# PEER stage of a decoder on one core: two of a tile's eight products of weights and activations on GpSimd instead of VectorE

## The reference

```python
q = (x @ Wq + bq).reshape(B, S, N_HEADS, D_QUERY)
s1 = jnp.einsum('bshd,nd->bshn', q1, K1)
s2 = jnp.einsum('bshd,nd->bshn', q2, K2)
v1, i1 = jax.lax.top_k(s1, TOPK)
v2, i2 = jax.lax.top_k(s2, TOPK)
...
vals, best = jax.lax.top_k(all_scores, TOPK)
expert_idx = jnp.take_along_axis(all_indices, best, axis=-1)
w_down = W_down[expert_idx]
w_up = W_up[expert_idx]
scores = jax.nn.softmax(vals, axis=-1)
h = jnp.einsum('bsd,bshkd->bshk', x, w_down)
h = jax.nn.gelu(h, approximate=False) * scores
out = jnp.einsum('bshk,bshkd->bsd', h, w_up)
```

## Time and profile before

| | |
|---|---|
| median of 3 runs | 3761.95 us (3757.82 to 3762.19) |
| profiled execution | 3762.07 us |
| its span | 3760.3 us |
| mean granted TensorE clock | 0.937 |
| busy over the span | PE 3271.3 (87%), PEld 2778.2 (74%), DVE 2726.7 (73%), ACT 1199.3 (32%), POOL 2150.9 (57%) |
| PEER's macros | about 972 to 2493 us of the span |

### The profile page before, as it was taken

The page is one execution under the profiler, slowest core; times in us unless marked ns, Lnnn a source line. Parts: engine busy times, 40 slices in busy tenths (PEclk is TensorE's granted clock), DMA queues, the critical chain, the costliest instruction groups (busy, mean ns, idle before and its releaser), DMA issues. The chain is left out here.

```text
span 3760.3 us, 93455 instructions
## 1 busy us (share of the span) xinstructions
PE 3271.3 (87%) x33694; PEld 2778.2 (74%) x33695; DVE 2726.7 (73%) x10805; ACT 1199.3 (32%) x3136; POOL 2150.9 (57%) x2456
## 2 busy tenths in 40 slices
PE   6999957876599999999999999978888799799998
PEld 4777735554488888888888888855555577699998
DVE  6666634544999999999999999948888467433333
ACT  1443425543222222222222222216665222122221
POOL 4444325551577777777777777768887233233333
PEclk9999978998799999999999999989999789799999
DMA  5444434443000000000000000024453231566665
GB/s 154 112 106 110 110 83 111 123 113 131 1 2 2 2 2 2 2 2 2 2 2 2 2 2 2 2 70 124 122 127 99 70 106 52 141 181 182 181 181 134
DMA packets 256260, 277.91 MB, mean 74 GB/s; under 512 B 44145, under 2 KB 200817, under 8 KB 255345
## 3 DMA queue, kind: packets, MB, share of 16 engines
q1 hardware_dynamic: 242225, 253.69, 23.5%
q0 software_dynamic: 13632, 18.91, 3.5%
HBM read 187.63 MB, written 72.29 MB: 69 GB/s over the span
## 5 line engine op out<-in xcount | busy, mean ns | idle before, releaser
L1190 POOL TENSOR_TENSOR peer_hot_v<-peer_hot_e,peer_parts 80x512 bf16<-80x512 bf16 x768 | 991.1, 1317 | 321.2 <-DVE peer_hot_e L1233 311.6
L1009 PE MATMUL peer_ps_u<-peer_up,peer_g 128*128 128x256 f32 x2048 | 533.5, 407 | 0.6 <-DVE x_all L1331 0.6
L990 PEld LDWEIGHTS peer_ps_h<-peer_xnT,peer_down 128*128 128x128 f32 x4096 | 513.4, 197 | 16.0 <-DMA peer_down<-in_peer_down 1.2
L990 PE MATMUL peer_ps_h<-peer_xnT,peer_down 128*128 128x128 f32 x4096 | 512.9, 280 | 1.0 <-DMA peer_down<-in_peer_down 1.0
L1000 PE MATMUL peer_ps_w<-peer_hot_v,peer_hot_u 80*128 80x32 bf16 x12288 | 347.3, 177 | 145.3 <-DVE peer_g L1245 98.6
L1000 PEld LDWEIGHTS peer_ps_w<-peer_hot_v,peer_hot_u 80*128 80x128 bf16 x12288 | 337.1, 97 | 167.4 <-issue 90.9
L1009 PEld LDWEIGHTS peer_ps_u<-peer_up,peer_g 128*128 128x128 f32 x2048 | 392.6, 201 | 53.2 <-issue 1.0
L1087 ACT ACTIVATE peer_g<-peer_ps_h 128x512 f32<-128x512 f32 x256 | 152.9, 597 | 842.3 <-PE peer_ps_h L990 842.0
L1237 DVE TENSOR_TENSOR peer_hot_u<-peer_count,peer_uvT 80x2048 bf16<-80x2048 bf16 x256 | 349.4, 1365 | 0.0
L2160 POOL DMA_INDIRECT out<-moe_y,moe_target x71 | 112.6, 1585 | 312.5 <-DVE moe_y L2261 309.6
L2104 PE MATMUL moe_ps_t<-moe_xgT,moe_w 128*128 128x128 f32 x2272 | 267.4, 276 | 0.0
(11 more groups left out here) (370 smaller groups left out, 7107.8 us busy)
## 6 DMA issues: line engine op xcount, KB each, us to landing
moe_w<-in_moe_w SPq DMA_DIRECT2D x142, 512.0 KB, 4.5
causal_qs<-causal_qscratch SPq DMA_DIRECT2D x32, 384.0 KB, 4.0
cross_qs<-cross_qscratch SPq DMA_DIRECT2D x32, 384.0 KB, 3.6
band_qs<-band_qscratch SPq DMA_DIRECT2D x32, 384.0 KB, 4.0
route_w<-in_moe_w SPq DMA_DIRECT2D x8, 1024.0 KB, 5.9
causal_qscratch<-causal_part SPq DMA_DIRECT2D x32, 192.0 KB, 2.6
causal_kscratch<-causal_part SPq DMA_DIRECT2D x32, 192.0 KB, 2.0
causal_ks<-causal_kscratch SPq DMA_DIRECT2D x32, 192.0 KB, 4.3
```

The source lines that it names most:

```text
L990: mm = nc.tensor.matmul(ps_h[:, n % 2, k * P:(k + 1) * P], down[:, c, 4 * n + k, :], xnT[:, par, c, :], start=(c == 0), stop=(c == DC - 1))
L1009: mm = nc.tensor.matmul(ps_u[:], g[:, par, v, :], up[:, v, :], start=(v == 0), stop=(v == EV - 1))
L1190: ins = nc.gpsimd.tensor_tensor(hot_v[0:SEL, n % RING, part], hot_e[0:SEL, n % RING], w, ALU.mult)
```

## The change

DVE's `weigh` returns at once for chunks 2 and 5 (`APART`). For these, ACT copies PE's bank to `wcopy` in SBUF (`take_w`), since POOL reads SBUF here, as the first thing of its turns 3 and 6. POOL's new `weigh` multiplies the copy into `g`, behind `hots` of turns 4 and 7. PE waits for a bank through `w_free`: for the copy where the bank's chunk was one of the two, otherwise for DVE's product, whose count is now 6 a tile. `output` waits for both counts. `take_w` waits until POOL has used the copy of the tile before. The diff:

```diff
--- before.py
+++ after.py
@@ -849,6 +849,8 @@
         stats.open(r)
         sb, ps, sem = r.sb, r.ps, r.sem
         SEL = NQ * TOP
+        APART = (2, 5)
+        HERE = NCH - len(APART)
         wq = sb("wq", [P, DC, 2 * NQ * HALF])
         bq = sb("bq", [P, 4])
         keys = sb("keys", [P, 2 * KEYS])
@@ -888,6 +890,7 @@
         hot_v = sb("hot_v", [P, RING, 3, CHUNK // 2, EV, 2], BF16)
         g = sb("g", [P, 2, EV, P])
         mark = sb("mark", [P, 1])
+        wcopy = sb("wcopy", [P, len(APART), 512])
 
         ps_q = ps("ps_q", [P, 512])
         ps_s = ps("ps_s", [P, 2, 512])
@@ -920,6 +923,8 @@
         v_ready = sem("v_ready")
         w_done = sem("w_done")
         gw_ready = sem("gw_ready")
+        w_copied = sem("w_copied")
+        gp_ready = sem("gp_ready")
         up_done = sem("up_done")
         x_used = sem("x_used")
         roots_ready = sem("roots_ready")
@@ -946,6 +951,17 @@
         def there(t):
 
             return not isinstance(t, int) or 0 <= t < TILES
+
+        def w_free(eng, t, n):
+
+            if n < 0:
+                t, n = t - 1, n + NCH
+            if t < 0:
+                return
+            if n in APART:
+                eng.wait_ge(w_copied, len(APART) * t + APART.index(n) + 1)
+            else:
+                eng.wait_ge(gw_ready, HERE * t + n + 1 - sum(k < n for k in APART))
 
         def by_pair(row, n):
 
@@ -994,7 +1010,7 @@
             def weights(t, n):
                 pe.wait_ge(u_ready, NCH * t + n + 1)
                 pe.wait_ge(v_ready, NCH * t + n + 1)
-                wait(pe, gw_ready, NCH * t + n - 1)
+                w_free(pe, t, n - 2)
                 for k in range(CHUNK):
                     for part in range(3):
                         mm = nc.tensor.matmul(ps_w[:, n % 2, k * EV:(k + 1) * EV], hot_u[0:SEL, n % RING, k // 2, :, k % 2],
@@ -1003,7 +1019,8 @@
 
             def output(t, par, a, b):
                 if a == 0:
-                    pe.wait_ge(gw_ready, NCH * (t + 1))
+                    pe.wait_ge(gw_ready, HERE * (t + 1))
+                    pe.wait_ge(gp_ready, len(APART) * (t + 1))
                     wait(pe, x_used, t)
                 for v in range(a, b):
                     mm = nc.tensor.matmul(ps_u[:], g[:, par, v, :], up[:, v, :], start=(v == 0), stop=(v == EV - 1))
@@ -1087,6 +1104,12 @@
                 nc.scalar.activation(g[:, par, 4 * n:4 * n + 4, :].rearrange("p v s -> p (v s)"), ps_h[:, n % 2, :],
                                      ACT.Gelu).then_inc(g_ready, 1)
 
+            def take_w(t, n):
+                k = APART.index(n)
+                act.wait_ge(w_done, NCH * t + n + 1)
+                wait(act, gp_ready, len(APART) * (t - 1) + k + 1)
+                nc.scalar.activation(wcopy[:, k, :], ps_w[:, n % 2, :], ACT.Copy).then_inc(w_copied, 1)
+
             def exps(t):
                 act.wait_ge(exp_in, t + 1)
                 for h in range(NQ):
@@ -1122,6 +1145,8 @@
 
             def macro(t, par):
                 for n in range(NCH):
+                    if n - 1 in APART:
+                        take_w(t, n - 1)
                     if there(t + 2):
                         if n == 1:
                             take_x(t + 2, par)
@@ -1190,6 +1215,12 @@
                     ins = nc.gpsimd.tensor_tensor(hot_v[0:SEL, n % RING, part], hot_e[0:SEL, n % RING], w, ALU.mult)
                 ins.then_inc(v_ready, 1)
 
+            def weigh(t, par, n):
+                k = APART.index(n)
+                pool.wait_ge(w_copied, len(APART) * t + k + 1)
+                gs = g[:, par, :, n * CHUNK:(n + 1) * CHUNK]
+                nc.gpsimd.tensor_tensor(gs, wcopy[:, k, :].rearrange("p (k v) -> p v k", v=EV), gs, ALU.mult).then_inc(gp_ready, 1)
+
             def first():
                 pool.wait_ge(roots_ready, 1)
                 norm(0)
@@ -1208,6 +1239,8 @@
                         hots(t, par, n + AHEAD)
                     elif there(t + 1):
                         hots(t + 1, 1 - par, n + AHEAD - NCH)
+                    if n - 2 in APART:
+                        weigh(t, par, n - 2)
                     if n == AGAIN:
                         steps.again()
 
```

## The result

The changed kernel takes 3815.18 us (median of 4 runs, 3813.04 to 3815.69), against 3762.07 us for the kernel before in the same comparison: a ratio of 1.0138, with a 95% interval of 1.0124 to 1.0151. The profiled execution has a span of 3813.3 us. I had forecast 3785 with a range up to 3815: slower was right, but the loss is +53 us where I had +23, just past the dear end of the range.

The account below looks back on a forecast made before the run. DVE was taken to set the PEER tile's period of 47.47 us. The terms -1.20 + 1.06 + 0.58 + 0.32 = +0.76 us a tile, times 30, gave 3762 + 23 = 3785, with a range from 3732 to 3815.

Parts of the forecast that it names:

- the walk of the two places: POOL's two new products placed among DVE's operations, DVE and POOL alternating: +1.06, +0.58 and +0.32 us a tile.
- a cover that just holds: DVE's need for ACT's scores: slack 0.68, losing 0.60 and some 0.3; counted as nothing, otherwise a few tenths a tile.
- The price of the product: POOL's new 128x512 product, taken as 1.26 us from the bias addition; dearest rate 2.44, skill's rule for stepped reads 1.9.
- the term for the candidates and the hot products: Chunk 5's product delays POOL's candidates into hot_e and hot_u of chunks 2 and 3 (+0.58), and chunk 4's (+0.32).
- DVE's idle time behind ACT: Sign of being wrong: DVE idle behind ACT or PE would be a wait that was taken for covered.
- What bounds the stage: In the PEER stage DVE, busy 46.25 of 47.47 us a tile, sets the period; PE waits for it.
- What leaves DVE: DVE's products of chunks 2 and 5 go, giving 2 x 0.60 = 1.20 us a tile.
- ACT's copies and PE's new waits: Two 128x512 copies out of PSUM in turns 3 and 6, and PE's waits for banks: cost on the path 0.
- Chunk 2's product at `choices`: POOL's product behind hots(t, 6) starts under 0.1 us ahead of DVE's first two-operand step; DVE loses 1.06 us.
- (a): Rival: POOL's products meet only DVE operations that don't care, so DVE does 1.20 less a tile: 3726; chance 0.20.
- (b): Rival: the collisions cost about what is saved, chunk 5's place coming out at its good phase: 3762; chance 0.14.
- (d): Rival: column-order reading makes POOL's product much dearer: 3802 at 1.85 us, 3820 at 2.44; chance 0.21.

Follow-up runs that it names:

- the row order: The changed kernel with ACT writing its copy in the order POOL reads it, timed against the kernel before: 3805.58 us, ratio 1.0126.

## Why the prediction was right in its direction and too small in its size

The step that failed is the walk of the two places. It set POOL's new products among DVE's operations and wrote at nothing what DVE meets when it comes earlier: the wait for the scores, called a cover that just holds, cost 0.45 a tile, `lookup` 0.30 and `places` 0.22. The price of the product was too low as well, which is another 0.22. Against these the term for the candidates and the hot products was 0.45 too high. That this hid a third of the errors is luck: without it the miss would have been 1.29 a tile instead of 0.84. The prediction had named DVE's idle time behind ACT as a sign of being wrong, and it came.

- **What bounds the stage**: right. DVE sets the period, and every kernel here follows DVE's blocked time and waits.
- **What leaves DVE**: 1.20 forecast, 1.22 measured.
- **ACT's copies and PE's new waits, cost 0**: right, by the kernel with the products left out.
- **Chunk 2's product at `choices`**: the mechanism and the place are right to 0.1 us. The term is 1.28, not 1.06, because the price was too low: I took the contiguous addition's 1.26 as the nearest row and named the column order as a doubt only. It measured 1.515, inside my two ends. 0.22 of the miss.
- **`lookup` and `places`**: missing from the forecast. I walked where POOL's new products fall, and did not walk what DVE's operations run into when they move forward by 0.6. The first step of `lookup` began 0.04 us ahead of the end of POOL's instruction, so a shift forward had to hit. It is 0.30 of the miss. The comparison in `places` is 0.22: 0.76 in 8 of 28 tiles, those in which chunk 4 loses least.
- **Scores**: the largest single part of the miss. I named this cover as thin (0.68 of slack, 0.60 and some 0.3 taken from it) and then wrote it at nothing. It costs 0.45 a tile in the mean: 0.17 in 8 of 28 tiles, 0.87 to 1.59 in 8 more, nothing in 12. What I couldn't see is that the lower clock can follow PE's wait, which turns a delay of 0.7 into one of 2.4 (the scores are there 16.83 us into the tile before the change, and 17.55 or 19.20 after it). The length of PE's wait alone doesn't decide it: the lower clock came behind 1.27 us with the products left out and not behind 2.10 in several tiles of the changed kernel.
- **Candidates and hot products**: 0.90 forecast, 0.45 measured (hot_e +0.34, hot_u +0.11). Its two parts came out the other way round. I walked one tile and took it for all. Rows 8 and 9 show a kind of tile that only 5 of 28 belong to (the four operations of chunks 2 and 3 lose 0.37, the two of chunk 4 1.31); in the other 23 hot_u of chunk 3 is the one that runs into hot_v, and the losses are 1.27 and 0.46, as the rows below show. After the change 24 tiles lose 0.60 to 0.79 in the first four and 0.9 or 1.6 in chunk 4, and four lose 2.7 to 2.9 in the first four and nothing in chunk 4. In the mean the first four went from 1.11 to 1.03 and chunk 4 from 0.61 to 1.18: -0.08 and +0.57 where I had +0.58 and +0.32. The timeline of DVE in the commoner tile of the kernel before:

```profile
1883.59 0.56 DVE L1233 TENSOR_TENSOR peer_hot_e<-peer_count,peer_uvT 80x512 bf16<-80x512 bf16 x1
1884.07 1.34 DVE L1237 TENSOR_TENSOR peer_hot_u<-peer_count,peer_uvT 80x2048 bf16<-80x2048 bf16 x1
1885.33 0.57 DVE L1233 TENSOR_TENSOR peer_hot_e<-peer_count,peer_uvT 80x512 bf16<-80x512 bf16 x1
1885.82 2.06 DVE L1237 TENSOR_TENSOR peer_hot_u<-peer_count,peer_uvT 80x2048 bf16<-80x2048 bf16 x1
...
1892.19 0.87 DVE L1233 TENSOR_TENSOR peer_hot_e<-peer_count,peer_uvT 80x512 bf16<-80x512 bf16 x1
1892.99 1.21 DVE L1237 TENSOR_TENSOR peer_hot_u<-peer_count,peer_uvT 80x2048 bf16<-80x2048 bf16 x1
```

- **The sum**: 1.06 + 0.90 = 1.96 of costs were forecast and 2.76 came (1.28 + 0.30 + 0.22 + 0.45 + 0.34 + 0.11 + 0.06); with 1.22 off, 1.54 for 0.76. The range ended at 3815 because its upper end came from a dearer product alone, and held no term for what I hadn't found.
- **Rivals**: (a) is out, by the kernel with the products left out; (b) is out, since 2.76 of costs stand against the 1.22 saved; (d) is right that the product is dearer and that it costs linearly, as the row order shows (-0.24 at `choices` for -0.25 of product), but it was a quarter of the miss (0.22 of 0.84) and not the whole.

## What to carry to other kernels

Work moved from VectorE to GpSimd is paid for by what VectorE wants while it runs: list the operations with two SBUF operands (and the small TENSOR_SCALARs) near its place, and give it a stretch of PSUM reads or sorting that is longer than itself. Walk it in several tiles and not in one. Then walk the other side too: everything behind the removed work moves forward, and an operation that began a few hundredths of a microsecond ahead of the end of the other engine's instruction will now run into it. A cover that is used up to within a tenth should be priced, with TensorE's lower clock level behind the gap as its upper end.

## What the runs showed of the hardware

- The lead needed to take the port is below 0.1 us: POOL's product, 0.08 to 0.09 ahead of DVE's step, wins in 30 of the 31 tiles that have both.
- The two directions are separate: a memset of 1.43 us on POOL leaves a two-operand TENSOR_TENSOR at 0.24 and holds a TENSOR_SCALAR for 1.22.
- Back-to-back POOL instructions of 0.3 us keep a waiting DVE operation out through up to five of them (hot_e 1.65 for 0.41); with a semaphore wait between them it is let in at once.
- POOL reading with a step of 128 bytes takes 1.515 for 1.269 us on 128x512.
- The granted TensorE clock fell to 0.50 behind a wait of PE of 1.27 us in 28 of 28 tiles of one kernel, and stayed at 1.00 behind 1.37 us in the kernel before.
